# A graph network kernel: seven instead of five node tiles of the convolutions summed by gathers, in order of degree

## The reference

```
x = x + attention_layer(relu(layernorm(x)), src, dst)        # 10 heads of 13, softmax over the edges into a node
h = relu(layernorm(x))
deg = edges into a node + 1;  dis = deg ** -0.5
conv(h, W, b)[i] = dis[i] * (sum over edges j->i of dis[j] * (h @ W)[j]  +  dis[i] * (h @ W)[i]) + b
h = relu(batchnorm(conv(h, W1, b1)));  h = relu(batchnorm(conv(h, W2, b2)))
h = relu(conv(h, W3, b3));  h = conv(h, W3, b3);  out = x + h
```

## Time and profile before

| | |
|---|---|
| time, median of 3 | 3773.18 us |
| the profiled execution, its time | 3790.5 us |
| its span | 3788.6 us |
| PE, PEld busy | 3354.5 us (89%), 2097.6 us (55%) |
| DVE, ACT, POOL busy | 2355.1 us (62%), 1776.8 us (47%), 2445.6 us (65%) |
| moved by DMA | 599.98 MB |

### The profile page before, as it was taken

How to read it: one execution, slowest core, us unless ns; L and a number is a source line. 1 busy time by engine, 2 the same in 40 slices (tenths; PEclk the granted TensorE clock), 3 DMA queues, 4 the chain that set the end, 5 groups by cost and what they waited for, 6 DMA issues and landing times. The chain is left out here.

```text
span 3788.6 us, 59184 instructions
## 1 busy us (share of the span) xinstructions
PE 3354.5 (89%) x20346; PEld 2097.6 (55%) x20346; DVE 2355.1 (62%) x3512; ACT 1776.8 (47%) x4853; POOL 2445.6 (65%) x2604
## 2 busy tenths in 40 slices
PE   5788888888888888888888787999999999999999
PEld 4566666666666666666655554444544454445444
DVE  8788888888888888888865574222422242224223
ACT  4788888888888878787744353000200020002000
POOL 2577777777777777777777001777277737764775
PEclk7688888888888888888887798999999999999999
DMA  7443334333333333334332415888688868877886
GB/s 207 125 108 103 107 104 107 104 107 104 107 104 107 104 107 104 107 104 124 103 85 60 62 51 169 254 254 256 215 255 254 253 215 254 256 248 229 259 264 192
DMA packets 491674, 599.98 MB, mean 158 GB/s; under 512 B 61546, under 2 KB 422613, under 8 KB 491103
## 3 DMA queue, kind: packets, MB, share of 16 engines
q1 hardware_dynamic: 355798, 337.71, 29.3%
q0 software_dynamic: 82960, 172.57, 18.4%
q10 hardware_dynamic: 52632, 86.13, 6.3%
HBM read 488.79 MB, written 109.00 MB: 158 GB/s over the span
## 5 line engine op out<-in xcount | busy, mean ns | idle before, releaser
L1001 POOL DMA_INDIRECT fts<-ft_tab,src_all x1568 | 1481.2, 945 | 477.7 <-issue 477.1
L2702 PE MATMUL cv_acc<-cv_cnt,cv_parts 128*128 128x512 bf16 x3960 | 864.0, 379 | 0.0
L2453 POOL DMA_INDIRECT cv_slots<-hs_tab,slot_idx x640 | 604.8, 945 | 195.1 <-issue 195.1
L1033 DVE TENSOR_TENSOR ohk<-iota_ps,key_cols 128x784 bf16<-128x784 f32 x704 | 651.1, 966 | 5.5
L2702 PEld LDWEIGHTS cv_acc<-cv_cnt,cv_parts 128*128 128x128 bf16 x3960 | 387.2, 98 | 464.6
L1457 PE MATMUL agg_ps<-terms,oh 128*64 128x141 f32 x2744 | 557.1, 378 | 75.6 <-DVE terms L1070 75.3
L1457 PEld LDWEIGHTS agg_ps<-terms,oh 128*64 128x64 f32 x2744 | 483.2, 189 | 116.3 <-DVE terms L1070 105.4
L1218 ACT ACTIVATE dist_l<-lo_iota,low 128x128 bf16<-128x128 f16 x1760 | 533.1, 387 | 16.5 <-ACT low L1213 0.4
L1397 PE MATMUL adj_ps<-ohk,ohl 128*128 128x196 bf16 x2816 | 378.2, 261 | 89.5 <-ACT strip L1270 46.8
L1270 ACT CAST strip<-adj_ps 128x392 bf16<-128x392 f32 x704 | 334.0, 474 | 239.5 <-PE adj_ps L1400 200.4
L2702 PE MATMUL cv_acc<-raw,cv_parts 128*128 128x512 bf16 x1920 | 420.9, 379 | 0.0
(11 more groups left out here) (350 smaller groups left out, 3592.1 us busy)
## 6 DMA issues: line engine op xcount, KB each, us to landing
cv_cnt<-adj SPq DMA_DIRECT2D x44, 2176.0 KB
cv_cnt<-adj SPq DMA_DIRECT2D x44, 2048.0 KB
raw<-adj SPq DMA_DIRECT2D x44, 2048.0 KB
adj<-strip ACTq DMA_DIRECT2D x176, 392.0 KB
fts<-ft_tab,src_all POOLq DMA_INDIRECT x1568
win<-ft_tab SPq DMA_DIRECT2D x196, 65.0 KB
hs_tab<-cv_hs ACTq DMA_DIRECT2D x24, 448.0 KB, 3.5
cv_slots<-hs_tab,slot_idx POOLq DMA_INDIRECT x640
```

The costliest lines, as they stand in the source:

```text
L1001: nc.gpsimd.indirect_dma_start(fts[u][:, k, :], None, ft_tab[:, :], bass.IndirectOffsetOnAxis(src_all[:, n, k:k + 1], 0)).then_inc(gathere ...
L1033: nc.vector.tensor_tensor(ohk[:, k.s, at, :], key_no.unsqueeze(1).to_broadcast([P, QC, KEYS]), columns(key_cols, k)[:, at].unsqueeze(2).to ...
L2453: nc.gpsimd.indirect_dma_start(slots[n % RING][:, e, :], None, hs_tab[:, :], bass.IndirectOffsetOnAxis(rows_at, 0)).then_inc(slots_in[n % ...
L2702: last = nc.tensor.matmul(a[:, 0:width], parts[:, r, b, :], cnt[q][:, 0:width // SUB, (b - b0) * SUB:(b - b0 + 1) * SUB], start=(b == 0 an ...
```

## The change

SPARSE goes from 5 to 7, so the last 7 tiles (896 nodes) are summed by gathers, and T0 from 44 to 42. DG stays 11, but the last group holds two tiles (NARROW) and is 256 columns wide. NSD, the number of strips, goes from 176 to 168.

To need no more slots than before, the 896 nodes are laid out by rank of their degree. `node_update` makes for each of them a key (degree x 1024 + number), counts on VectorE how many keys are smaller (`ranks`), scatters start, degree and number of each node to its place (`list_tab`), reads them back and builds the slot lists on GpSimd. Tile k of the ranked nodes gets CAPS[k] slots. The highest tile is laid out in falling order, so that its fullest node shares 66 slots with the emptiest node of the lowest tile: the first 36 slots belong to the high one alone, slots 36 to 60 to either (two masks say whose), the rest to the low one. In all NSLOT = 236 gathers in 29 blocks.

In the convolutions the last tile piece's product comes fifth instead of last. Its rows go to `sorted_tab` in memory, GpSimd gathers them in ranked order (7 gathers, 14 in the first layer), SP stores them to `hs_tab`, ScalarE and VectorE make the parts from them, and only then the slot gathers start. In the last layer the ranked sums go back through `sorted_tab` and 7 gathers before x is added.

```diff
+PRODUCTS = TILES[:4] + TILES[7:] + TILES[4:7]
-SPARSE = 5
+SPARSE = 7
-SLOTS = 48
-SB = 8
...
+PAIR, ALONE, MOST = 66, 36, 60
+CAPS = (PAIR - ALONE, 29, 32, 34, 36, 39, MOST)
+SB = 9
...
-DG = T0 * P // GRP
+DG = -(-T0 * P // GRP)
+NARROW = T0 - (DG - 1) * GT
...
+        def keys_across(sp):
+            sp.wait_ge(s["key_made"], 1)
...
+                sp.dma_start(key_tab.rearrange("(t p) -> p t", p=P), key[:]).then_inc(s["key_out"], 16)
+            sp.wait_ge(s["key_out"], 16)
+            sp.dma_start(key_row, row_bc(key_tab)).then_inc(s["key_row_in"], 16)
...
             sp.dma_start(hT[:, 0:FT * P], hT_tab).then_inc(s["early_in"], 16)
+            keys_across(sp)
             sp.wait_ge(s["dis_made"], 1)
-            factors(sp)
+            first_factors(sp)
+            sp.wait_ge(s["slot_const"], 1)
+            sp.dma_start(hs_tab[NP:TAB, :], no_row[:]).then_inc(s["pad_out"], 16)
+            lists_back(sp)
             later_hn(sp)
...
+            def ranks():
+                dve.wait_ge(s["key_row_in"], 16)
+                for k in range(SPARSE):
...
+                    nc.vector.tensor_scalar(lower[k % 2], key_row, key[:, k:k + 1], None, ALU.is_lt
+                                            ).then_inc(s["below_made"], 1)
+                    dve.wait_ge(s["below_made"], k + 1)
+                    nc.vector.tensor_reduce(rank[:, k:k + 1], lower[k % 2], AX.X, ALU.add
+                                            ).then_inc(s["below_summed"], 1)
...
+                    if i == MANY - 1 and not redo:
+                        last_roots()
+                    if i == MANY and not redo:
+                        final_flag()
...
+            def last_rows(l, places):
+                pool.wait_ge(s["sorted_out"], 16 * (l + 1))
+                for k in range(SPARSE):
+                    nc.gpsimd.indirect_dma_start(last_hs[:, k, :], None, sorted_tab[:, :],
+                                                 bass.IndirectOffsetOnAxis(places[:, k:k + 1], 0)
+                                                 ).then_inc(s["last_in"], 16)
...
+                    for e in range(block.size):
+                        for k, mine in ((SPARSE - 1, of_top), (0, of_low)):
+                            step = nc.vector.scalar_tensor_tensor(sums[:, k, :], slots[r][:, e, :],
+                                                                  mine[:, block.at + e:block.at + e + 1], sums[:, k, :],
+                                                                  ALU.mult, ALU.add)
...
+                act.wait_ge(s["last_in"], 16 * SPARSE * (l + 1))
+                nc.scalar.copy(parts[:, 0, T0:, :], last_hs).then_inc(s["first_part"], 1)
...
-                        group(l, l * DG + i, acc[i % 2], i * GT, GRP, turn_sums if i == DG - 1 else None)
+                        if i < DG - 1:
+                            group(l, l * DG + i, acc[i % 2], i * GT, GRP)
+                        elif l < L - 1:
+                            group(l, l * DG + i, acc[i % 2], i * GT, NARROW * P, {NT - 8: turn_sums})
+                        else:
+                            group(l, l * DG + i, acc[i % 2], i * GT, NARROW * P,
+                                  {NT - 30: turn_sums, NT - 20: lambda: turn_rows(DG - 2), NT - 8: lambda: turn_rows(DG - 1)})
```

More of the change, by code:

```diff
@@ new lines, in slot_lists @@
+            pool.wait_ge(s["list_in"], 16)
+            start, deg, node = (lists[:, :, j] for j in range(3))
+            top, low = deg[:, SPARSE - 1:SPARSE], deg[:, 0:1]
+            nc.gpsimd.tensor_copy(own_idx[:], node)
+            nc.gpsimd.tensor_tensor(wrapped[:], deg, caps[:], ALU.subtract)
+            nc.gpsimd.tensor_tensor(turned[:, 0:1], top, low, ALU.add)
+            nc.gpsimd.tensor_copy(slot_start[:, 1:], start[:, 1:])
+            nc.gpsimd.tensor_scalar(turned[:, 2:3], low, -1.0, float(PAIR), ALU.mult, ALU.add)
@@ new lines, in slot_lists @@
+            link(nc.gpsimd.tensor_tensor(turned[:, 1:2], start[:, 0:1], low, ALU.add))
+            nc.gpsimd.tensor_scalar(over[:, 0:SPARSE], wrapped[:], 0.0, None, ALU.is_gt)
+            nc.gpsimd.tensor_scalar(over[:, SPARSE:SPARSE + 1], turned[:, 0:1], float(PAIR), None, ALU.is_gt)
+            nc.gpsimd.tensor_scalar(over[:, SPARSE + 1:SPARSE + 2], turned[:, 1:2], float(PAIR), None, ALU.is_lt
+                                    ).then_inc(s["over_made"], 1)
+            link(nc.gpsimd.tensor_scalar(turned[:, 3:4], turned[:, 1:2], -float(PAIR), 0.0, ALU.add, ALU.max))
@@ L2186, in _ @@
                         factor_roots()
+                    if i == MANY - 2 and not redo:
+                        last_factor_roots()
                     if there(i + 1):
@@ L2302, in convolutions, with slots_landed @@
     LATE = 3
+    LAST = PRODUCTS.index(TILES[-1])
+    rows_of = [k for k in range(NW) if k != LAST]
+    stores = (4, 3)
+    landed = [sum(b.size for b in SLOT_BLOCKS[r::RING]) for r in range(RING)]
+    def slots_landed(l, b):
+        r = b % RING
+        return 16 * (l * landed[r] + sum(SLOT_BLOCKS[j].size for j in range(r, b + 1, RING)))
     with ExitStack() as c:
@@ L2492, in add_more @@
                     if n:
                         dve.wait_ge(s["slots_used"], n)
-                    dve.wait_ge(slots_in[n % RING], 16 * SB * (n // RING + 1))
-                    nc.vector.tensor_reduce(extra, slots[n % RING][:, 0:SB, :].rearrange("p e d -> p d e"), AX.X, ALU.add
-                                            ).then_inc(s["slots_used"], 1)
-                    dve.wait_ge(s["slots_used"], n + 1)
-                    for k in range(SPARSE):
-                        last = nc.vector.scalar_tensor_tensor(sums[:, k, :], extra, more[:, k:k + 1], sums[:, k, :],
-                                                              ALU.mult, ALU.add)
@@ L2750, in _ @@
                         for r in range(3):
[L2751 removed]
+                            last = nc.tensor.matmul(acc[0][:, 0:P], rows[:, r, :], oh, start=(r == 0), stop=(r == 2))
                         last.then_inc(s["part_ps"], 1)
```

450 lines of the change are left out of this document (308 added, 142 removed).

## The result

The changed kernel takes 3754.03 us (median of five, 3753.53 to 3755.52), the kernel before beside it 3775.25 (3769.32 to 3780.04): a ratio of 0.9946 with an interval of 0.9931 to 0.9960, some 21 us faster. The same two kernels timed once more gave 0.9934 (0.9916 to 0.9951), 3754.03 against 3775.59. The forecast was 3732: faster, but by twice as much.

What follows compares the result with a forecast made beforehand. Bounds: GpSimd gathers in attention, VectorE in node update, TensorE in convolutions. Terms -14.5 + 6.5 - 33.3 + 0.6 = -40.7 us, taken off the median 3773.18, gave 3732; own range 3716 to 3748, with two rivals 3712 to 3758.

Steps and rivals of the forecast that it cites:

- node update: Between attention and convolutions: seven comparisons and sums on VectorE, waiting for keys, delay the statistics; +6.5 us, range +2 to +12.
- layers one to three: Convolutions: each layer -15.5 for narrow matmuls, +3.9 for the first group, +0.5 for finishing tiles; together -33.3 us.
- last layer: From the last group to the span's end 37.6 us instead of 40.9, -3.3; with +3.9 of the first group, +0.6.
- attention term: End of the attention: eight light steps after the heavy ones win back 1.8 us each of 20 us lateness, -14.5 us.
- My first rival: End of the attention: light steps stay at gather pace and win nothing back, so -14.5 becomes 0; 3747 us, chance 0.12.
- two rivals: Late attention steps win nothing back, 3747 us, chance 0.12; the last piece's parts come late in each layer, 3756, chance 0.12.
- The two operations of the ranks: Node update on VectorE: a comparison of 896 elements 0.62 us, a sum 1.17; seven of both 12.5 us.
- The keys' way: Node update: keys made on GpSimd at about 2125, stored in 3.1 us, read back to VectorE at about 2134.5.
- A narrow pair: Convolutions' last group: a weight load and 256 columns take 0.110 us instead of 0.2158, saving 15.5 us a layer.
- the first group: Each layer's first group has one piece less in hand, so TensorE waits: +3.9 us a layer, range +1 to +6.
- The rule of the Trainium skill: Convolutions: loads overlap matmuls only across different row groups, so narrow pairs would save nothing; the weight-load rival, 3790 us, chance 0.03.
- The hand-off: Convolutions: the last piece's store, gathers and landing finish at 2710, 3 us before ScalarE needs them at about 2713.

Runs made afterwards that it cites:

- b2: The kernel before, unchanged, traced a third time: a single execution of 3773.19 us.
- b1: The kernel before, unchanged, run and traced again: twelve executions from 3774 to 3791 us, median 3780.6.
- e3: The kernel before with only the attention's part: 168 strips, node update units eight steps earlier; 3777.41 us against 3775.59, ratio 0.9996.
- e1: The changed kernel with the four node update units starting at step 176 as before: 3772.09 us, ratio 0.9966 to the kernel before.
- a1: The changed kernel, unchanged, timed and traced once more: median 3754.03 us against 3775.59 for the kernel before.
- e5: The changed kernel with the last group's matmuls 512 columns wide again, transfers still narrow: 3812.41 us, 58.4 over the changed kernel.

## Why the prediction was wrong

By its own steps, against the execution that it was read from:

| us | forecast | measured against that execution | against b2 |
|---|---|---|---|
| attention, to step 195's product | -14.5 | -19.2 | -0.9 |
| node update | +6.5 | +12.4 | +11.7 |
| layers one to three | -33.3 | -32.3 | -32.5 |
| last layer | +0.6 | +2.3 | +2.1 |
| sum | -40.7 | -36.8 | -19.6 |

**The step that failed is the attention term, together with the carrying over to the median.** I read a lateness of 20 us from one execution that was 17 us over the median, took it for the kernel's, and then took the same -40.7 off the median, as if the 17 us lay somewhere that the change doesn't touch. They lay in the very steps that it moves. b1 and b2 show the lateness at 7 and 2 us, with the granted clock at 0.87 and 0.89 where the forecast's execution had 0.72, and e3 shows no gain of the median by the moved steps alone. The mechanism was right (e1, 12 to 18 us for putting the units back; a1, the scatter gone). Against the forecast's execution it was even worth more than I took, 19.2 us, since the first light steps of the changed kernel ran at 6.1 to 7.4 us, not at 8.2. My first rival had the right number for the median, 3747 and 6 more of node update, for a wrong reason: not that light steps win nothing back, but that there is mostly nothing to win. The measured 3754 lies outside the forecast's own 3716 to 3748. It lies inside the wide range, 3712 to 3758, only because that was drawn to take in two rivals, and neither came about as argued.

**The node update was mis-sized at +6.5, measured +12.4 (+11.7 against b2).** The two operations of the ranks were right (0.69 and 1.09 against 0.62 and 1.17). The keys' way was not: I priced the store by its elements at 3.5 ns, 3.1 us for 896 values, from a store of 6272. From the issue of the store to the issue of the read it took 2117.38 - 2107.66 = 9.7 us, and the rows were there 3.7 later. The keys themselves were made 8.6 us behind the stage's start, not 6.7. So the ranks started 22.0 us behind the stage's start, not 16. I kept +12 as the end of the range; it was the value.

**The convolutions were right.** A narrow pair 0.109 (forecast 0.110), the first group 3.8 us longer (3.9), with the two waits where I put them, 0.94 for 1.1 and 2.50 for 2.4; layers one to three 10.7, 11.6 and 10.0 us shorter (11.1). The rule of the Trainium skill ("TensorE: Matmul & The Clock Gate", Part 3, that a weight load overlaps matmuls in flight only across different row groups) doesn't hold for these pairs: 5.24 us for 48 with a load of 98 ns in each, all on the same rows, and e5's 58 us. The hand-off waited for nothing; only the slot gathers began 5.5 us later in the layer instead of 1.2, behind the last store to `hs_tab`, which the slack of the turning took up. The last layer's end gained 4.6 us (3.3), but its first group lost 6.9 instead of 3.9 (3426.08 - 3372.57 = 53.5 us to the next group, 3458.24 - 3411.63 = 46.6 before), and 2.70 us of that are the second of these rows, a wait of TensorE in the middle of its second product for which the profile shows no releaser:

```profile
3375.73 1.02 PE L2968 MATMUL cv_w_ps<-cv_W,raw 128*128 128x128 f32 x7 [1.16 <-issue]
3379.45 1.66 PE L2968 MATMUL cv_w_ps<-cv_W,raw 128*128 128x128 f32 x7 [2.70 <-issue]
```

It stands in all seven traces of the changed kernel and its variants, 1.79 to 3.04 us. In the kernel before the product has no such wait in its middle, only 0.3 us ahead of it. What it is isn't settled.

## What to carry to other kernels

Before a term is read from one execution, compare its time with the median: if they differ, find the stretch where, for a change to that stretch can't be taken off the median. In this kernel the heavy last steps, on the engine with a varying clock, gave a tail that showed in the scatter; light steps behind them bought a narrow spread and next to no median. And work that must wait for a trip through memory belongs where its engine waits anyway, one operation at a time: seven pairs in a row cost 12 us, spread they cost 5.

## What was not expected of the hardware

A store of one value per transfer element does not cost by its count: from its issue to the issue of the read that waits for it 896 values took 8.4 to 10.1 us and 5376 values 20.2 to 23.5 over the seven traces of the changed kernel and its variants, 6272 values 21.8 to 24.0 over the five of the kernel before and its. b1's is the longest:

```profile
2137.80 0.37 SPq L1875 DMA_DIRECT2D dis_tab<-dis_col  x1
2161.79 0.32 SPq L1877 DMA_DIRECT2D dis_row<-dis_tab  x1
```

It is 24.0 us, and the load of `nu_hnT` queued behind it on SP is what TensorE then waits for. And equal code on equal data met a mean granted clock between 0.72 and 0.89 in the same 65 us of three traces, 1980 to 2045; one execution doesn't tell which it will be.
